# Identity products on TensorE ahead of and around the first batch of a cross-attention and LoRA kernel

## What is computed

```python
def _L0_xattn_ref(query, key):
    a = jnp.einsum('bqd,bkd->bqk', query, key)
    e = jax.nn.softmax(a, axis=-1)
    c = jnp.einsum('bqk,bkd->bqd', e, key)
    return c
...
x = x + _L0_xattn_ref(_layernorm(x, axis=-1), ctx_4096)
x = x + _L0_ffn_ref(_layernorm(x, axis=-1), base_w, base_b, A, B, router_w)
```

## Time and profile before

| | |
|---|---|
| median of three runs | 1354.93 us (1353.49 to 1358.51) |
| the profiled execution's own time | 1358.12 us |
| its span, first to last instruction | 1356.3 us |
| mean granted TensorE clock | 0.998 |
| TensorE matmul busy | 1324.6 us, 6567 records |
| VectorE busy | 969.1 us |
| ScalarE busy | 600.2 us |
| GpSimd busy | 335.9 us |

### The profile page before, as it was taken

One profiled execution on the slowest core, in us unless ns is written; L12 is line 12 of the kernel. 1 busy time (PEld: TensorE's weight loads), 2 busy tenths in 40 slices (PEclk: granted clock), 3 DMA queues, 4 the chain that ended last, 5 costly groups with the idle time before them and its releaser, 6 DMA issues.

```text
span 1356.3 us, 16807 instructions
## 1 busy us (share of the span) xinstructions
PE 1324.6 (98%) x6567; PEld 1081.9 (80%) x6567; DVE 969.1 (71%) x1235; ACT 600.2 (44%) x763; POOL 335.9 (25%) x233
## 2 busy tenths in 40 slices
PE   5999999999999999999999999999999999999998
PEld 4778788887878788887888887888787888888887
DVE  5588888889798888879475467777777555455554
ACT  3346554645546464546222367777776211111110
POOL 2003012120302112121615723454442111111110
PEclk9999999999999999999999999999999999999999
DMA  8986978788796977769557598999995977877874
GB/s 299 267 317 218 299 245 250 245 263 271 229 301 212 285 261 244 249 226 199 193 164 212 176 294 282 316 325 298 325 254 183 325 258 250 271 248 264 255 266 153
DMA packets 159598, 345.66 MB, mean 255 GB/s; under 512 B 51680, under 2 KB 68064, under 8 KB 145760
## 3 DMA queue, kind: packets, MB, share of 16 engines
q1 hardware_dynamic: 140928, 277.06, 64.4%
q0 software_dynamic: 10528, 52.85, 12.4%
q10 hardware_dynamic: 8064, 14.68, 3.0%
HBM read 260.87 MB, written 99.41 MB: 266 GB/s over the span
## 4 chain that ended last, share of the span: by engine, by line
PE 75%; DVE 10%; DMA 7%; ACT 4%; issue 2%; POOL 1%; SPq 0%; ACTq 0%; DVEq 0%; POOLq 0%
PE scores L920 12%; PE scores L922 12%; PE scores L921 12%; PE scores L889 6%; PE scores L891 6%; PE scores L890 6%; PE scores L776 4%; PE scores L778 4%; PE scores L777 4%; DMA y_scratch<-y_out,yrow_i 3%; DVE ctxT_l L1258 3%; DVE raw_l L1268 2%; PE work L956 2%; PE work L957 2%; DVE st L1273 1%
## 5 line engine op out<-in xcount | busy, mean ns | idle before, releaser
L920 PE MATMUL scores<-w_h,a_h 128*128 128x512 f32 x896 | 351.3, 392 | 1.3 <-DVE w_l L1532 1.3
L922 PE MATMUL scores<-w_h,a_l 128*128 128x512 f32 x896 | 350.4, 391 | 0.0
L921 PE MATMUL scores<-w_l,a_h 128*128 128x512 f32 x896 | 349.9, 391 | 0.0
L1133 ACT ACTIVATE a_h<-a_in 128x512 fp32r<-128x512 f32 x148 | 83.6, 622 | 311.8 <-DMA a_in<-xT_scratch 209.9
L920 PEld LDWEIGHTS scores<-w_h,a_h 128*128 128x128 f32 x896 | 168.0, 188 | 38.8 <-DVE w_l L1532 1.7
L922 PEld LDWEIGHTS scores<-w_h,a_l 128*128 128x128 f32 x896 | 168.0, 188 | 37.5
L921 PEld LDWEIGHTS scores<-w_l,a_h 128*128 128x128 f32 x896 | 168.1, 188 | 36.9
L1050 ACT ACTIVATE val_h<-raw_in 128x512 fp32r<-128x512 f32 x192 | 120.2, 629 | 126.9 <-PE scores L891 126.9
L776 PE MATMUL scores<-ctxT_h,nT_h 128*112 128x494 f32 (+1 forms) x512 | 174.4, 341 | 1.6 <-DVE nT_l L1254 1.1
L777 PE MATMUL scores<-ctxT_l,nT_h 128*112 128x494 f32 (+1 forms) x512 | 171.7, 335 | 0.0
L778 PE MATMUL scores<-ctxT_h,nT_l 128*112 128x494 f32 (+1 forms) x512 | 171.6, 335 | 0.0
(11 more groups left out here) (161 smaller groups left out, 1963.7 us busy)
## 6 DMA issues: line engine op xcount, KB each, us to landing
ctxT_in<-in_ctxT_dram SPq DMA_DIRECT2D x64, 750.0 KB, 4.4
raw_in<-in_ctx_dram SPq DMA_DIRECT2D x32, 1280.0 KB
a_in<-xT_scratch SPq DMA_DIRECT2D x37, 1024.0 KB, 7.1
w_in<-in_wT_dram SPq DMA_DIRECT2D x32, 512.0 KB, 7.3
y_add<-y_scratch SPq DMA_DIRECT2D x56, 256.0 KB, 6.8
late_y<-y_scratch SPq DMA_DIRECT2D x56, 256.0 KB, 6.6
nT_in<-in_xT_dram SPq DMA_DIRECT2D x7, 1792.0 KB, 10.2
res<-x_scratch SPq DMA_DIRECT2D x42, 256.0 KB, 5.8
```

The source lines that it names most:

```text
L920: pe.matmul(o, ah, wh, start=(k == 0), stop=False)
L921: pe.matmul(o, ah, wl, start=False, stop=False)
L922: last = pe.matmul(o, al, wh, start=False, stop=(k == KD - 1))
```

## The change

TensorE's list gets 63 matmuls more, each the 128x128 float32 identity times itself, started and stopped on its own, into columns of PSUM that are overwritten before anything reads them. 48 stand after the wait for the identity and before the first transposes. 7 stand in the first batch's `exps_T` between the six transposes of half 0 and the wait for the exponentials of half 1; a `take`, the wait for the PSUM slot, is put ahead of them (it asks for what was already drained by then). 8 stand before the wait at the head of the first batch's `outputs_of`. No other engine's list is changed, no semaphore is added, and no transfer.

```diff
@@ -54,6 +54,8 @@
+SPIN_START = 48
+SPIN_SOFTMAX, SPIN_VALUES = (0, 7), 8
@@ -765,6 +767,11 @@
+            def spin(out, times):
+
+                for _ in range(times):
+                    pe.matmul(out, ident[:, :], ident[:, :], start=True, stop=True)
+
@@ -859,6 +866,9 @@
             def exps_T(stage, b):
                 for q in range(NQ):
+                    if stage == "first":
+                        take(job_no(stage, b, "eT", q))
+                        spin(place(stage, "eT", q)[:, 0:P], SPIN_SOFTMAX[q])
                     pe.wait_ge(exp_done, b * NQ + q + 1)
                     take(job_no(stage, b, "eT", q))
                     slot = slot_of(stage, "eT", q)
@@ -870,6 +880,8 @@
             def outputs_of(stage, b):
 
+                if stage == "first":
+                    spin(scores[:, 0, 0:P], SPIN_VALUES)
                 pe.wait_ge(drained, job_no(stage, b, "eT", NQ - 1) + 1)
@@ -977,6 +989,7 @@
             pe.wait_ge(ident_ready, 2)
+            spin(scores[:, 1, 0:P], SPIN_START)
             first_rows(0)
             first_rows(1)
             one(0, "first")
```

## The result

The changed kernel takes **1361.87 us** (median of 22 executions, 1354.26 to 1373.02), beside 1357.48 us for the kernel before (22 executions, 1353.49 to 1360.5): a ratio of 1.0038, 95% interval 1.0026 to 1.0049. The forecast of 1354.4 us was wrong, and its range of 1351.0 to 1357.5 does not hold the result. The result lies 7.5 us above the forecast. Of these, 2.6 us are due to the first three executions of before, whose median lay that much under that of 22; 0.5 us are the gain that was forecast and did not come; 4.4 us are a loss that the forecast did not have. The ratio lies within the 0.5% that the forecast gave 0.94, but its interval leaves out 1, and so the sign was wrong.

A forecast was written before the change was run, and what follows sets the result against it. TensorE is supplied nearly always, so only its low-clock pace could improve: -0.5 us (start) + 0 (softmax) = -0.5 us, against the median of 1354.93 giving 1354.4 us, range 1351.0 to 1357.5.

The forecast's parts named there:

- The spins' cost and end: At the start: 48 identity products, 0.217 us each at full clock, end at 14.2 us, hidden, costing nothing.
- c: Microseconds of low clock during the start's 48 identity products: 4.4 taken, 3.45 and 8.6 as farther values.
- Does the clock last until 19.33?: Gap before the first score product: clock falls near 19.5 us, returns near 22.95; gain 0.5 us.
- the first rival: The clock holds through the gap at the start: gain 2.0 instead of 0.5 us, 1352.9 us; chance 0.20.
- a sign of being wrong: Score step 0 at the start taking 4.2 us would show the forecast wrong.
- 2.0 us "at most": Most that can be won at the start: step 0 took 6.22 us, step 1, the same products, 4.21.
- The softmax: First softmax: 7 and 8 identity products hidden, no clock fall at 61.40, TensorE 1.7 us further on by 65.
- What is late next: Block 18 near 87 us: TensorE waits for VectorE behind `nT_in`; nothing of the softmax's 1.7 us is left.
- It moves only with what started the full stretch: The `nT_in` transfer lands earlier only through the start's shift, so the start's 0.5 us pass block 18.
- nothing, and 1.7 us: Bounds on what is left of the softmax's gain at block 18; 1.7 if the transfer lands that much earlier.
- the second rival: The softmax's gain survives block 18: gain 0.5 + 1.7, 1352.7 us; chance 0.17, alone or with the first rival.
- The slower rival: The start's identity products stay at low clock, first product 6.7 us later: 1361.6 us; chance 0.08.

The follow-up runs named there:

- after_again: The changed kernel unaltered, measured again beside before: 1362.11 us, ratio 1.0021.
- after_third: The changed kernel unaltered, measured once more beside before: 1361.55 us, ratio 1.002.
- start_only: The changed kernel with only the 48 identity products at the start, those of the softmax left out: 1359.35 us, ratio 1.0012.
- fed_wait: The changed kernel plus 8, 3 and 2 identity products ahead of blocks 15, 16 and 18 of the first batch: 1359.76 us, ratio 1.002.
- after_xt: The changed kernel with the `nT_in` transfer issued ahead of batch 1's transposed context: 1357.26 us, ratio 0.9989.
- after_pad36: The changed kernel plus 36 idle instructions between the first transposes and the first score product: 1361.56 us, ratio 1.0035.
- before_xt: The kernel before, no identity products, with the `nT_in` transfer issued ahead of batch 1's transposed context: 1357.71 us, ratio 1.0001.
- pad_nops: The kernel before with 252 idle instructions at the head of TensorE's list: 1356.25 us, ratio 0.9991.
- start39_fill9: The changed kernel with 39 identity products at the start instead of 48, and 9 behind the first transposes: 1360.18 us, ratio 1.0016.
- before_late: The kernel before with the `nT_in` transfer issued at 71.22 us instead of 56.51: 1363.91 us, ratio 1.0051.

## Why the prediction was wrong

- **The spins' cost and end** were right in size: 0.219 us against 0.217. They ended at 15.5, not 14.2 (c was 6.1 us, inside its bounds), and they were hidden: the first product came at 19.53 instead of 19.33.
- **Does the clock last until 19.33?** Forecast: no, and a gain of 0.5 us. With 48 spins and an open gap it held in five traces (the profiled execution, `after_again`, `after_third`, `start_only`, `fed_wait`): that is the first rival with its 2.0 us, and step 0 at 4.20 us was a sign of being wrong that the prediction had named. It fell in `after_xt` (19.73) and `after_pad36` (18.99, which has idle instructions in the gap). The forecast took one row for what happens every time. Its 2.0 us "at most" also took one execution of before for all: in `before_xt` and `pad_nops` nothing had run on TensorE but the 16 transposes when the clock column first rose, at 18.83 and 18.43 us, and step 0 ran at full rate. The rule of the Trainium skill on transposes (TensorE: Matmul & The Clock Gate, Part 4) is not borne out by these two, and with the same 16 transposes in the gap behind spins the clock held and fell.
- **The softmax** was right: spins hidden, no low stretch, and the 1.7 us there.
- **What is late next** named the right place, VectorE's row behind `nT_in`, and said rightly that the softmax's gain ends there. **Its failing step is the transfer**: "It moves only with what started the full stretch", so that "The 0.5 us of the start thus pass", with the ends "nothing, and 1.7 us". A start 1.3 to 1.8 us earlier gave landings at 79.93, 82.24 and 83.22 against 80.15: the transfer took 25.1, 26.5 and 27.4 us from its issue where it had taken 23.6. I took that time as fixed, the second rival let it vary only as a gain, and a loss was shut out.
- **The second failing step is what a lead turns into.** A lead of 2 to 3 us in front of a transfer that does not come earlier is a wait of that length, and I priced that as the gain returned. In `after_again`, `after_third`, `start39_fill9` and `before_late` the clock fell around such a wait of 3.0 to 4.0 us and stayed low for 3.41 or 6.83 us. In `after_again` the wait took 3.2 us from where TensorE stood and the low clock another 2.6. Rows 5 and 6 of before showed this mechanism at the softmax; I used it there and not at block 15.
- **A place that the prediction did not look at** is the load of `xn` near 440 us: 2.2 us in the profiled execution, 0.9 and 2.3 us in `after_again` and `after_third`. No run isolates its share of the 4.4 us.
- **The slower rival** had its time near the result, 1361.6 us against 1361.87, and that is luck: its spins stay at the low clock and hold up the first product, while here they ran at 0.219 us apiece from 7.74 us on and held up nothing.
- Against the measurement of before beside it, the change costs 4.4 us. `before_late` shows a late landing with its wait and low clock to cost 6.0 us with no spin (1363.91 against 1357.90), and with an early landing (`after_xt`) no cost of the change is seen. What makes the landing late is not isolated.

## What to carry to other kernels

Before crediting an engine with time won ahead of a full DMA stretch, ask what happens if the transfer at its end lands 2 us later, not only if it lands as before; where an engine already waits for that transfer, 0.85 us here, that is the question that sets the sign. A lead that meets a fixed arrival becomes one long wait, and in five traces here a wait of TensorE of 2.3 to 4.0 us had half the clock in it or right behind it. Where matmuls are added only to hold the clock, time two or three counts of them: between 48 and 57 the time here differed by more than the spins could win.

## What was not expected of the hardware

- A DMA issue on SyncE's queue takes 0.43 us, and took 1.04 to 1.50 us in the eight traces where it overlapped the read of a 16384-byte piece of a program.
- Matmuls added at the start move those reads (33.8 to 35.6 us with 48 of them, 31.6 to 33.1 with 57, 41.85 with 39), and nine products of 0.22 us went with 6 us of the whole: 1355.96 us with 57 spins, 1361.87 with 48, in different sets. With idle instructions the reads stood as in before.
- Sixteen transposes alone had the full clock behind them in `before_xt` (18.83 us) and `pad_nops` (18.43 us), and not in four other traces with the same start (22.73 to 25.22 us).
- The clock column reads 1.00 over the spins up to 7.74 that stood 0.42 us apart, as it did over before's slow first step.
